# Attention and routed experts on one core: all engines' orders written anew, and two groups of filler products left out

## What is computed

```python
mod = (silu(c) @ wmod)                       # sa, ca, ga, sb, cb, gb for each sequence
h = layernorm(x) * (1 + ca) + sa
q, k, v = split(rms_norm(h) @ w_qkv.T)       # q, k normalized again
w = cumsum(exp(k)); kv = cumsum(exp(k) * v)  # along the sequence
y = sigmoid(q) * kv / (w + 1e-6)
u, g = split(y @ w_swiglu.T)
x = x + ga * (h + (u * silu(g)) @ w_out.T)
h = layernorm(x) * (1 + cb) + sb
gate = h @ gate_w.T                          # 16 experts, top 1, capacity 320
# each token goes to a row (expert, rank); h1 = gelu(row @ w1[e]); row_out = h1 @ w2[e]
x = x + gb * prob * row_out                  # tokens over capacity get nothing
```

## Time and profile before

| what | value |
|---|---|
| time, median of 3 runs | 205.05 us (204.35 to 205.32) |
| the profiled execution | 206.09 us, of it the span of the profile 204.2 us |
| busy in the span | TensorE 94%, VectorE 73%, ScalarE 71%, GpSimd 60% |
| chain that ended last | TensorE 78%, ScalarE 7%, GpSimd 4% |
| project_out(7) ends | 102.46 us |
| first expert product | 124.76 us |

### The profile page before, as it was taken

The page is one execution under the profiler, slowest core; times in us unless marked ns, Lnnn a source line. Parts: engine busy times, 40 slices in busy tenths (PEclk is TensorE's granted clock), DMA queues, the critical chain, the costliest instruction groups (busy, mean ns, idle before and its releaser), DMA issues.

```text
span 204.2 us, 4070 instructions
## 1 busy us (share of the span) xinstructions
PE 191.0 (94%) x1189; PEld 157.0 (77%) x1189; DVE 148.2 (73%) x467; ACT 145.1 (71%) x424; POOL 123.0 (60%) x154
## 2 busy tenths in 40 slices
PE   7998999999999999999968999999999999999960
PEld 4888778689888988777745568797888879787950
DVE  2658989999999999989972855284766756685530
ACT  4478999999999999888664835586584857553400
POOL 6232646274558888788776770505775845685774
PEclk9999999999999999999987999999999999999997
DMA  4999999979701332332499574996959575410110
GB/s 141 289 336 360 359 356 356 307 272 259 214 3 51 116 96 77 129 119 105 136 308 397 197 193 147 334 334 195 309 168 357 178 212 169 148 45 31 37 31 14
DMA packets 38597, 40.26 MB, mean 197 GB/s; under 512 B 2623, under 2 KB 32646, under 8 KB 38576
## 3 DMA queue, kind: packets, MB, share of 16 engines
q1 hardware_dynamic: 35248, 32.94, 51.4%
q0 software_dynamic: 3328, 7.07, 9.7%
HBM read 19.85 MB, written 19.94 MB: 195 GB/s over the span
## 4 chain that ended last, share of the span: by engine, by line
PE 78%; ACT 7%; POOL 4%; issue 4%; DVE 3%; DMA 2%; POOLq 1%; DVEq 0%; ACTq 0%
PE bank L1353 15%; PE bank L1339 12%; PE bank L1104 6%; PE bank L1122 4%; PE bank L1143 4%; PE bank L1148 4%; PE bank L1157 3%; POOL out_dram L568 3%; PE bank L1159 3%; PE bank L1115 3%; PE bank L1213 3%; PE bank L1174 2%; PE bank L1094 2%; ACT junk L599 2%; PE bank L1288 2%
## 5 line engine op out<-in xcount | busy, mean ns | idle before, releaser
L568 POOL DMA_INDIRECT out_dram<-x_all,rest x40 | 42.8, 1069 | 26.6 <-DVE x_all L1050 13.9
L531 POOL DMA_INDIRECT dispatched_rows<-rows,slot x32 | 32.5, 1016 | 10.1 <-issue 8.7
L748 ACT ACTIVATE HT<-bank 128x320 f32<-128x320 f32 x64 | 28.0, 438 | 10.6 <-PE bank L1339 10.2
L1353 PE MATMUL bank<-HT,w 128*128 128x320 f32 x112 | 32.4, 432 | 0.0
L1353 PEld LDWEIGHTS bank<-HT,w 128*128 128x128 f32 x112 | 20.7, 190 | 6.6
L1339 PE MATMUL bank<-xth,w1h 128*128 128x320 f32 x64 | 22.5, 352 | 0.0
L1339 PE MATMUL bank<-xtl,w1h 128*128 128x320 f32 x64 | 19.8, 309 | 0.0
L1339 PE MATMUL bank<-xth,w1l 128*128 128x320 f32 x64 | 19.8, 309 | 0.0
L1069 DVE COPY OT<-bank 128x320 f32<-128x320 f32 x14 | 6.9, 492 | 16.1 <-PE bank L1353 16.1
L599 ACT ACTIVATE junk<-bank 128x128 f32<-128x128 f32 x64 | 16.7, 306 | 2.3 <-PE bank L1104 2.3
L508 POOL TENSOR_TENSOR hsq<-hT 128x512 f32<-128x512 f32 x8 | 8.3, 1043 | 15.6 <-ACT hT L320 13.7
(11 more groups left out here) (178 smaller groups left out, 501.5 us busy)
## 6 DMA issues: line engine op xcount, KB each, us to landing
dispatched_rows<-blank SPq DMA_DIRECT2D x9, 965.0 KB, 12.8
w<-in_L_ffn_w_dram SPq DMA_DIRECT2D x16, 512.0 KB, 7.4
rest<-dispatched_rows SPq DMA_DIRECT2D x8, 645.0 KB, 5.5
hin<-dispatched_rows SPq DMA_DIRECT2D x7, 320.0 KB, 5.9
x_all<-in_L_attn_x_dram SPq DMA_DIRECT2D x8, 256.0 KB, 5.1
rows<-gb_row SPq DMA_DIRECT2D x8, 256.0 KB, 4.0
out_dram<-rows SPq DMA_DIRECT2D x8, 256.0 KB, 3.3
x_all<-dispatched_rows SPq DMA_DIRECT2D x1, 645.0 KB, 4.5
```

Of the source, the lines that this page charges most:

```text
L531: pool.indirect_dma_start(out=disp_d, out_offset=bass.IndirectOffsetOnAxis(ap=slot[:, b, j:j + 1], axis=0), in_=rows[:, b, j, :], in_offse ...
L568: pool.indirect_dma_start(out=out_d.rearrange("b t d -> (b t) d"), out_offset=bass.IndirectOffsetOnAxis(ap=rest[i % RING][:, n, C_TOK - D: ...
L748: act.activation(HT[e][:, f, :], ps_h[c % HB][:, 0:CAP], ACT.Gelu_apprx_tanh).then_inc(h_done, 1)
L1353: last = pe.matmul(ps_o[e], w2[i % RING][:, e, f, :], HT[e][:, f, :], start=(f == 0), stop=(f == NF - 1))
```

## The change

All four orders are written anew. The steps are the same, apart from who does some of them: modulate1(3) goes from VectorE to ScalarE and modulate2(0) from ScalarE to VectorE; normalize2(2) from GpSimd to ScalarE, normalize2(3) from ScalarE to GpSimd, normalize2(7) from ScalarE to VectorE; weigh_sums(1) and (3) from VectorE to GpSimd, (2) and (5) from GpSimd to VectorE; silu(0), (2), (5) from GpSimd to VectorE, silu(1) and (6) from VectorE to GpSimd. One of nine run_late fillers is gone, and of the three keep_running the first two. Lines behind the orders of ScalarE and TensorE move up by one or more.

```diff
-            squares(0); normalize1(pool, 1); squares(1); normalize1(pool, 3); squares(2)
-            weigh_sums(pool, 0); squares(3); normalize1(pool, 4); silu(pool, 0); number_slots()
...
+            weigh_sums(pool, 0); normalize1(pool, 4); squares(3); squares(4); weigh_sums(pool, 1)
+            normalize1(pool, 5); number_slots(); silu(pool, 1); normalize2(pool, 0); squares(5)
...
             claim(pe, "kv", o_done, 0)
-            keep_running(512)
             pe.wait_ge(h2_done, NB)
             near_rows(0)
             near_rows(1)
             pe.wait_ge(scattered, 16 * (NB - 1 - FIRST) * NJ)
-            keep_running(384, 2)
             far_rows()
             keep_running(256)
```

More of the change, by code:

```diff
@@ L693, in _ @@
             ln1_scale(3); rms_scales(1); exp_k(1); exp_q(1); log_denominator(0); keep_row(0)
[L694 to L709, removed]
@@ L984, in _ @@
             stats1(3); modulations(); diagonal(0); weigh_v(0); normalize1(dve, 2); aggregate1(3)
[L985 to L998, removed]
-            scan_w(7); weigh_v(7); denominator(7); residual(4); top_prob(2); stats2(4); aggregate2(4)
@@ L1005, in _ @@
-            top_prob(6); slots(6); top_value(7); top_expert(7); top_prob(7); slots(7); last_slots(7)
-            hot_slots()
+            h_means(1); qk_means(1); scan_w(0); modulate1(dve, 2); shift1(3); denominator(0); stats1(4)
+            scan_kv(0); weigh_v(1); aggregate1(4); scan_w(1); shift1(4); h_means(2); qk_means(2)
+            clamp_g(0); scan_kv(1); diagonal(1); denominator(1); stats1(5); h_means(3); silu(dve, 0)
+            gate_u(0); aggregate1(5); stats1(6); weigh_v(2); qk_means(3); residual(0); shift1(5)
@@ new lines, in _ @@
+            stats2(0); clamp_g(1); scan_w(2); aggregate1(6); denominator(2); h_means(4); aggregate2(0)
+            stats1(7); scan_kv(2); scan_w(3); gate_u(1); weigh_sums(dve, 2); shift2(0); weigh_v(3)
+            qk_means(4); shift1(6); denominator(3); residual(1); stats2(1); clamp_g(2); modulate2(dve, 0)
+            aggregate2(1); h_means(5); aggregate1(7); scan_kv(3); top_value(0); weigh_v(4); top_expert(0)
+            silu(dve, 2); shift2(1); gate_u(2); shift1(7); qk_means(5); clamp_g(3); top_prob(0); scan_w(4)
@@ new lines, in _ @@
+            residual(2); denominator(4); stats2(2); scan_kv(4); aggregate2(2); scan_w(5); shift2(2)
+            weigh_v(5); gate_u(3); denominator(5); slots(0); top_value(1); h_means(6); top_expert(1)
+            qk_means(6); top_prob(1); clamp_g(4); residual(3); scan_kv(5); stats2(3); slots(1)
+            aggregate2(3); scan_w(6); shift2(3); weigh_v(6); denominator(6); gate_u(4); weigh_sums(dve, 5)
+            top_value(2); h_means(7); top_expert(2); qk_means(7); scan_kv(6); clamp_g(5); top_prob(2)
```

85 lines of the change are left out of this document (51 added, 34 removed).

## The result

The changed kernel is **slower by 3.1%**: 211.69 us (210.73 to 212.27) against 205.19 us for the kernel before, ratio 1.031 with a 95% interval of 1.024 to 1.037. Run a second time beside 23 executions of the kernel before, it gave 211.12 against 205.71 us, ratio 1.029 (1.023 to 1.035). The direction was the one forecast, the size wasn't: +6.5 us where +2.1 was said, and outside the range.

The account below looks back on a forecast made before the run. Three full engines (TensorE, VectorE, ScalarE) were taken to bound the attention pipeline, then one chain to the first expert product. Lag +3.4 less fillers 1.3 gave +2.1 us: 207.1 us median, range 204.5 to 209.0.

Parts of the forecast that it names:

- The start, swap of project_v(0): At the start, project_v(0) queued behind project_qk(1) delays weigh_v(0) to about 19.7 us and makes qk_means(1) 2.0 us later.
- transpose1(3) ahead of project_qk(2): At the start, project_qk(2) waits behind transpose1(3) for GpSimd's xh: start at 27.0 instead of 23.44 us, 3.6 us later.
- The lag carried to project_out(7): From the start to the last batch, a lag of 3.4 us stays at project_out(7), with 1.0 and 4.0 as ends.
- Rivals 1 and 3: Attention pipeline: idle time repays lag partly (205.4 us; 0.22 together with GpSimd's rival) or wholly (203.7 us; 0.13).
- The durations at the start: At the start, project_qk(1) followed by project_v(0)'s 1.59 us of weight loads and 1.08 us: 16.95 to 19.6 us.
- The fillers' -1.3 us: Ahead of far_rows, leaving out the fillers lets it start when its rows land: 1.3 us gained, at most 1.7.
- rival 2: Ahead of far_rows, lag kept and clock falls in the gap, costing 1.2 us (0.8 to 1.7): 208.3 us; chance 0.20.
- Rival 4: GpSimd's scatters set the end, 28.9 us from weigh_sums(7) to first expert product: 205.4 to 206.1 us; 0.22 with rival 1.

Follow-up runs that it names:

- e4: Changed kernel with both groups of fillers around the one-hot products put back: 209.24 us, ratio 1.010 to the kernel before.
- e5: Changed kernel as it is, run once more in six executions: 211.12 us, ratio 1.029 to the kernel before.
- e9: Kernel before with a 384-column filler in each of two TensorE waits behind project_out(7), the one behind logits(6) dropped: 204.01 us, ratio 0.994.
- e13: Changed kernel with both groups of fillers put back, run again with more executions: 208.16 us, ratio 1.013 to the kernel before.
- e14: Changed kernel with only the pair of 384-column fillers between near_rows and far_rows put back: 210.0 us, ratio 1.014 to the kernel before.

## Why the prediction was wrong

**The start, swap of project_v(0): right, and the largest term.** weigh_v(0) was put at 19.7 us and qk_means(1) at 22.4; where the clock is full they are at 19.72 and 22.61 (e4) and 19.87 and 22.76 (e5). The swap costs 2.3 us to project_out(7), where the prediction had 2.0 at qk_means(1). weigh_v(0) in the timeline of VectorE in e4:

```profile
19.72 1.13 DVE L801 SCALAR_TENSOR_TENSOR ewkv<-bank,nrr,ewkv 128x128 f32<-128x128 f32 x4 [2.81 <-PE bank L1114]
```

**transpose1(3) ahead of project_qk(2): right at its place.** 27.0 was said, 27.20 (e4) and 27.36 (e5) measured. Its 1.6 us were half given back, to 0.7 or 0.8.

**The lag carried to project_out(7): right for the order.** 3.4 us were taken, 3.8 measured at full clock, in the bounds. That the two lie so close is in part luck: the wait for transpose1(3) counted half of what was said, and 0.8 us are the middle batches', for which the prediction took nothing. Rivals 1 and 3, by which idle time pays the lag back, are out: scan_kv(7) ended at 97.50 us, not at 87.8, and project_out(7) is 3.8 us later with the clock's falls taken off.

**The durations at the start: the first step that failed.** The sum took project_qk(1) and project_v(0) at full clock, from the rows of a trace in which it was full there. In the profiled execution they ran at half, 2.3 us more; in the second one the clock fell at 82 us, 1.5 us more. So project_out(7) ended at 108.54 and 107.74 us, where 105.5 to 106.5 were said. The prediction weighed the clock at one place only, ahead of far_rows, and had no term for falls elsewhere.

**The fillers' -1.3 us: the second step that failed, though its number came out.** To the first expert product it is 21.0 us instead of 22.3, just the 1.3 that was said. The cause was another. The kernel before had the fall at 106 us in this stretch, 1.7 us by e9, and the changed kernel hadn't. The changed order had already put near_rows 3 us earlier against the transfer, so that with the fillers in the stretch is 20.5 us: far_rows starts 18.3 us behind project_out(7) with them (e13) and without them, and leaving them out gained nothing. In the second execution of the changed kernel even the number is gone, with 22.4 us. Leaving them out opened a wait, and behind that came rival 2's fall. That rival was given 0.20 and 1.2 us; it came in each of the five traces, and it reached into the experts, which the sum took as untouched: from the first expert product to the end it is 80.1 and 81.1 us instead of 79.4. Fillers out against fillers in: 1.9 to 3.5 us in the medians.

Together, the spans of the two profiled executions differ by 5.5 us: 3.8 for the order, 2.3 for the clock at the start, 1.3 less to the first expert product, 0.7 in the experts. The sum had 3.4 - 1.3 = 2.1 of these; of the 3.4 us that it lacks, 0.4 are the order's and 3.0 the clock's. Another 0.7 us of the difference in time lies outside the spans and isn't explained.

**Rival 4, GpSimd: its path was there.** What sets the start of the transfer of hin in the changed kernel is GpSimd as much as the slots. From weigh_sums(7) on, its counts and scatters follow each other to the end of scatter(6) with no idle time above 0.5 us, and scatter(5) ends at 116.32 us, just as slot(6) is written, at 116.26. GpSimd's weigh_sums(7), slot(6) on VectorE, and the first piece of scatter(6):

```profile
98.38 1.28 POOL L287 TENSOR_TENSOR yT<-kvsum,rden 128x512 f32<-128x512 f32 x1
...
116.10 0.16 DVE L909 SCALAR_TENSOR_TENSOR slot<-bank,sl_a 128x4 int32<-128x4 f32 x1
...
117.13 0.99 POOL L531 DMA_INDIRECT dispatched_rows<-rows,slot  x1 [0.47 <-issue]
```

In the kernel before, GpSimd waited 1.32 us for slot(6) at this place:

```profile
111.43 0.99 POOL L531 DMA_INDIRECT dispatched_rows<-rows,slot  x1 [1.32 <-DVE slot L910]
```

From the end of weigh_sums(7) to the first expert product it is 29.9 us in the changed kernel and 29.3 in e13, where rival 4 said 28.9; its time was too low since weigh_sums(7) ended at 99.7 us, not at 96 to 97. No run separates the two paths, so which of them binds stays open.

**What stays open.** Why the clock falls in one execution at 15 us, in another at 82, and in a third (e13) nowhere from 5 to 202 us, with the same instructions ahead. The longest wait of TensorE in the 3 us ahead of the fall at 15 us is 0.32 us (at 13.20), ahead of that at 82 us in e5 0.24, less than the 2.07 us that e13 had ahead of project_qk(1) with the clock staying full. That the place differs between executions of one kernel is shown; what decides it isn't.

## What to carry to other kernels

Before a filler on TensorE is taken out, look at what the next product waits for: if that is a transfer, the filler stands in the wait and costs nothing, and taking it out can halve the clock for the products behind it (1.9 to 3.5 us in the medians here); if it is the filler itself, taking it out gains its length (1.3 us in the traces, too little to be clear in the times). A product with its operands ready that stood ahead of one that had to wait was free here, and the swap of the two cost more than its own time (2.3 us for 1.05 us of products), since the engine that reads it then waited for both. And where the clock in a trace of the kernel before is down anywhere, its place is chance as well as order: the sum needs a term, with a chance, for a fall in other stretches too, not only in the one that the change opens.

## What the runs showed of the hardware

The clock's falls move. The traces of these kernels show it at half at 8, 12, 14 to 21, 82, 90, 106 and 121 to 133 us in different combinations, and executions of the kernel before lie at 203.15 us with a mean granted clock of 0.995 and at 205.9 with one of 0.985. The Trainium skill says as much of the start of a kernel ("TensorE: Matmul & The Clock Gate", "What's actually happening": the number of slow products differs from execution to execution); here it holds for falls in the middle too. Falls had prices that could be read between two milestones: 1.5 us at 82 us, 1.7 at 106, and at 15 us 2.3 in the changed kernel, where it lasted to 21.6 us, but 0.3 in e14, where it ended at 17.6. The record of the clock begins only at 10.5 us in the trace of the kernel before, and a stage ahead of that is shown as full: four transposes of 128 columns at 7.06 us took 1.09 us there, and 0.66 us at 6.77 in e13.
